# Folding the second attention's weights inside the first expert layer's routing, and mixing expert rows on VectorE

## The reference, cut to what matters

```
x = x + tanh(g_ffn[0])   * L0_ffn(layernorm(x))      # 64 experts, top 3
x = x + tanh(g_xattn[1]) * L1_xattn(layernorm(x))    # 16 heads of 64

L0_ffn:  logits = x @ gate_w + gate_b;  top 3, gates = softmax(top 3)
         pos = running count of tokens per expert;  valid = pos < 64
         buf[expert, pos] = x
         y = gelu(buf @ w1 + b1) @ w2 + b2            # per expert
         out[token] = sum over k of y[expert_k, pos_k] * gate_k * valid_k
L1_xattn: q = x @ Wq; k = ctx @ Wk; v = ctx @ Wv
         out = softmax(q k^T / 8) v, heads joined, @ Wo + bo
```

## Time and profile before

| | us |
|---|---|
| median of 3 runs | 4144.75 |
| lowest and highest run | 4140.34, 4147.81 |
| profiled execution, its own time | 4137.59 |
| its span in the profile | 4136.0 |
| mean granted TensorE clock | 0.924 |

### The profile page before, as it was taken

The page is one execution under the profiler, slowest core; times in us unless marked ns, Lnnn a source line. Parts: engine busy times, 40 slices in busy tenths (PEclk is TensorE's granted clock), DMA queues, the critical chain, the costliest instruction groups (busy, mean ns, idle before and its releaser), DMA issues. The chain is left out here.

```text
span 4136.0 us, 84598 instructions
## 1 busy us (share of the span) xinstructions
PE 3638.2 (88%) x33128; PEld 2481.3 (60%) x33128; DVE 2430.1 (59%) x3802; ACT 2047.4 (50%) x2959; POOL 1527.6 (37%) x1887
## 2 busy tenths in 40 slices
PE   8499999946489999989999997679958799999997
PEld 8367777733366666666666665257733366666664
DVE  7556666543245554515454542467644799999993
ACT  8177777711134443434443442166422377777764
POOL 5265545221423233213323220022201577666651
PEclk9699999968789999999999997889969699999998
DMA  6177777546223332213333220021000566666650
GB/s 188 49 170 178 176 167 175 145 182 235 52 71 90 84 91 81 80 51 87 81 87 87 83 78 26 10 64 46 13 19 16 123 145 144 140 140 147 145 120 15
DMA packets 202294, 421.94 MB, mean 102 GB/s; under 512 B 51993, under 2 KB 108244, under 8 KB 201844
## 3 DMA queue, kind: packets, MB, share of 16 engines
q1 hardware_dynamic: 131524, 327.92, 31.2%
q0 software_dynamic: 34944, 46.10, 5.1%
q10 hardware_dynamic: 35504, 43.39, 3.9%
HBM read 232.39 MB, written 32.56 MB: 64 GB/s over the span
## 5 line engine op out<-in xcount | busy, mean ns | idle before, releaser
L1512 DVE TENSOR_REDUCE L_mp<-ps 128x2 f32<-128x1000 f32 (+1 forms) x352 | 402.4, 1151 | 560.7 <-PE ps L1310 557.3
L1347 PE MATMUL ps<-L_p,L_cn 125*97 125x448 f32 x1536 | 639.2, 538 | 0.0
L1494 ACT ACTIVATE L_p<-ps 125x896 f32<-125x896 f32 x384 | 352.1, 917 | 533.8 <-PE ps L1335 462.5
L2291 DVE TENSOR_REDUCE L_mp<-ps 112x1 f32<-112x500 f32 x726 | 454.2, 667 | 64.5 <-PE ps L2040 64.4
L1333 PE MATMUL ps<-L_qh,L_ch 97*125 97x448 f32 x768 | 384.4, 501 | 0.0
L1347 PEld LDWEIGHTS ps<-L_p,L_cn 125*97 125x97 f32 x1536 | 250.4, 163 | 199.9 <-issue 165.9
L2241 ACT ACTIVATE L_p<-L_p 125x896 f32<-125x896 f32 x256 | 243.3, 950 | 178.6 <-DVE L_p L2308 178.0
L2308 DVE TENSOR_SCALAR L_p<-ps 125x896 f32<-125x896 f32 x256 | 276.5, 1080 | 24.6 <-PE ps L2061 24.5
L920 ACT ACTIVATE L_p<-ps,rk 125x896 f32<-125x896 f32 x256 | 257.7, 1007 | 50.9 <-PE ps L776 46.8
L1334 PE MATMUL ps<-L_ql,L_ch 96*125 96x448 f32 x768 | 282.3, 368 | 0.0
L1335 PE MATMUL ps<-L_qh,L_cl 96*125 96x448 f32 x768 | 280.8, 366 | 0.0
(11 more groups left out here) (538 smaller groups left out, 7632.6 us busy)
## 6 DMA issues: line engine op xcount, KB each, us to landing
L_ks<-L_k_part SPq DMA_DIRECT2D x288, 375.0 KB, 6.1
L_ks<-L_k_first SPq DMA_DIRECT2D x96, 375.0 KB, 5.2
moe_w<-in_L_w SPq DMA_DIRECT2D x64, 512.0 KB, 6.6
L_cn<-in_ctxN SPq DMA_DIRECT2D x32, 568.4 KB
cs_ct<-in_ctxT SPq DMA_DIRECT2D x32, 562.5 KB, 4.2
L_cr<-in_ctxT POOLq DMA_DIRECT2D x32, 562.5 KB
L_ch<-in_ctxT POOLq DMA_DIRECT2D x32, 562.5 KB, 4.5
L_raw<-in_ctxT SPq DMA_DIRECT2D x32, 562.5 KB, 5.1
```

The source lines that it names most:

```text
L1347: mm = nc.tensor.matmul(U[:, a, :], CN[s][:, j, :], P[:, n % 2, a * HALF:(a + 1) * HALF], start=(j == 0), stop=(j == KT - 1))
L1494: nc.scalar.activation(two(P[:, n % 2, :]), SB[n % 2], ACT.Exp).then_inc(S["exped"].sem, 1)
L1512: nc.vector.tensor_reduce(mp[:, 2 * k:2 * k + n], ps[:, bank:bank + n, 0:500], AX.X, ALU.max).then_inc(S["chunk_maxed"].sem, 1)
L2291: nc.vector.tensor_reduce(mp[:, 2 * c + a:2 * c + a + 1], ps[0:TT, CB[0].start + a, 0:500], AX.X, ALU.max).then_inc(S["chunk_maxed"], 1)
```

## The change

The fold block goes. `M`, `N` and `cq` are allocated before `experts0` and filled inside its routing block. The L1 weights are loaded into the last two of the 14 expert slots, which are not yet loaded: WqT and WkAT on partitions 0 to 63 of `moe_w1` and `moe_w2`, Wo and WvA on partitions 64 to 127. SP issues these five loads after the gate loads and before the zero stores; it loads the last two slots' expert weights only after `folded` has reached 5. PE does the fold and the cq columns after its 14 turns and before it waits for `routed` and counts. ACT copies the folded banks to `M` and `N` and scales cq, ahead of its three exponentials. The layer norm `a1` runs without loads beside it.

In the mixing block the diagonals and their matmuls go. When a group's rows have landed, DVE multiplies them with the gates and adds them up (five instructions a group, in `mix`), PE turns the sum (14 transposes in all), and DVE adds it to `xT` (in `add`). DVE does `add(g)` before `mix(g + 1)`.

```diff
-def fold_weights(core, L, M, N, cq, scale, keep_max, dh, values, norm=None):
...
-def attention_wide(core, L, src, bo, scale, bit, image, norm):
+def attention_wide(core, L, src, bo, scale, bit, image, folded, held):
...
-        fold_weights(core, L, M, N, cq, scale, True, 64, None, norm)
...
+FOLD_BANKS = (6, 2, 4, 6)
...
+            def unfolded(t, p, n):
+                return t[p:p + DH1, NS - 2:NS, :, :].rearrange("p s e n -> p (s e n)")[:, 0:H * n].rearrange(
+                    "p (h n) -> p h n", n=n)
+            wqt, wka = unfolded(w1, 0, D), unfolded(w2, 0, KA)
+            wo, wva = unfolded(w1, DH1, D), unfolded(w2, DH1, KA)
...
+                    for dst, name in ((wqt, "WqT"), (wka, "WkAT"), (wo, "Wo"), (wva, "WvA"), (bqh[:, :], "bqh")):
+                        sp.dma_start(dst, d[f"L1_{name}"]).then_inc(S["fold_in"], 16)
                     sp.wait_ge(S["zeroed"], 1)
...
                     for s in range(NS):
+                        if s == NS - 2:
+                            sp.wait_ge(S["folded"], 5)
                         load_weights(sp, s, s)
...
+                    pe.wait_ge(S["fold_in"], 80)
+                    pe.wait_ge(S["rows_copied"], 1)
+                    for g in range(4):
+                        if g == 3:
+                            pe.wait_ge(S["fold_placed"], 2)
+                        for k in range(4):
+                            h = 4 * g + k
+                            nc.tensor.matmul(ps[:, FOLD_BANKS[g], k * KA:(k + 1) * KA], wqt[:, h, :], wka[:, h, :],
+                                             start=True, stop=True)
+                            mm = nc.tensor.matmul(ps[0:KA, FOLD_BANKS[g] + 1, k * D:(k + 1) * D], wva[:, h, :],
+                                                  wo[:, h, :], start=True, stop=True)
+                        mm.then_inc(S["folded"], 1)
+                    pe.wait_ge(S["fold_placed"], 4)
+                    for h in range(H):
+                        mm = nc.tensor.matmul(ps[0:KA, FOLD_BANKS[1], h:h + 1], wka[:, h, :], bqh[:, h:h + 1],
+                                              start=True, stop=True)
+                    mm.then_inc(S["folded"], 1)
                     pe.wait_ge(S["routed"], 1)
...
+                    for g in range(4):
+                        act.wait_ge(S["folded"], g + 1)
+                        nc.scalar.activation(M[:, 4 * g:4 * g + 4, :].rearrange("p h n -> p (h n)"),
+                                             ps[:, FOLD_BANKS[g], 0:4 * KA], ACT.Copy).then_inc(S["fold_placed"], 1)
...
+                    act.wait_ge(S["folded"], 5)
+                    nc.scalar.activation(cq[:, :], ps[0:KA, FOLD_BANKS[1], 0:H], ACT.Copy, scale=scale)
                     act.wait_ge(S["exp_in"], 1)
...
+                    def mix(g):
...
+                        dve.wait_ge(S[f"gathered{g}"], 16 * TOPK0 * len(tiles))
+                        nc.vector.tensor_tensor(mixed[:, u, :], yr[0][:, u, :], gates(0), ALU.mult)
...
-                                mm = nc.tensor.matmul(ps[:, g, (t % 4) * TT:(t % 4 + 1) * TT], yr[k][:, t, :],
-                                                      by_gate[k][:, t, :], start=(k == 0), stop=(k == TOPK0 - 1))
+                            mm = nc.tensor.transpose(ps[:, g, (t % 4) * TT:(t % 4 + 1) * TT], mixed[:, t, :],
+                                                     core.ident[:, :])
...
-        attention_wide(core, "L1", core.xn, v(core, "L1_bo"), 0.125, bit, image, norm1)
+        layer_norm(core, core.xT, core.xn, "a1")
+        attention_wide(core, "L1", core.xn, v(core, "L1_bo"), 0.125, bit, image, folded, held)
```

More of the change, by code:

```diff
@@ L437 @@
 QV = H // 4 * NQ
-def fold_weights(core, L, M, N, cq, scale, keep_max, dh, values, norm=None):
[L442 to L502, removed]
-                if keep_max:
-                    dve.wait_ge(m_mm.sem, 2)
-                    nc.vector.tensor_scalar(cq[:, :], ps[0:KA, 0, 0:H], scale, None,
-                                            ALU.mult).then_inc(m_sb.sem, 1)
@@ L2420, in experts0 @@
     C4 = HID0 // 128
+    M, N, cq = folded
+    DH1 = 64
     with ExitStack() as ctx:
@@ L2752, in experts0 @@
             yr = [sb(f"yr{k}", [TT, NT, D], c=c3) for k in range(TOPK0)]
-            by_gate = [sb(f"by_gate{k}", [TT, NT, TT], c=c3) for k in range(TOPK0)]
+            mixed = sb("mixed", [TT, NT, D], c=c3)
+            part = sb("part", [TT, 2, 4, D], c=c3)
             groups = [range(g, min(g + 4, NT)) for g in range(0, NT, 4)]
             S = {n: core.sig(f"moe_{n}").sem for n in [f"gathered{g}" for g in range(len(groups))]
-                 + ["gates_act", "gates_dve", "mix_turned"]}
+                 + ["mixed", "mix_turned"]}
             with nc.Block() as block:
@@ L2766, in _, with gates, add @@
                                     bounds_check=R - 1, oob_is_err=False).then_inc(S[f"gathered{g}"], 16)
-                @block.scalar
-                def _(act):
-                    for t in range(NT):
-                        nc.scalar.activation(by_gate[0][:, t, :], core.ident[:, :], ACT.Copy,
-                                             scale=gat[0][:, t:t + 1]).then_inc(S["gates_act"], 1)
                 @block.vector
                 def _(dve):
-                    for t in range(NT):
-                        for k in range(1, TOPK0):
-                            nc.vector.tensor_scalar(by_gate[k][:, t, :], core.ident[:, :], gat[k][:, t:t + 1], None,
-                                                    ALU.mult).then_inc(S["gates_dve"], 1)
-                    for g, tiles in enumerate(groups):
+                    link = core.linker(dve, "dve")
+                    def mix(g):
+                        tiles = groups[g]
+                        u = slice(tiles[0], tiles[-1] + 1)
+                        def gates(k):
+                            return gat[k][:, u].unsqueeze(2).to_broadcast([TT, len(tiles), D])
+                        dve.wait_ge(S[f"gathered{g}"], 16 * TOPK0 * len(tiles))
+                        nc.vector.tensor_tensor(mixed[:, u, :], yr[0][:, u, :], gates(0), ALU.mult)
+                        for k in (1, 2):
+                            ins = nc.vector.tensor_tensor(part[:, k - 1, 0:len(tiles), :], yr[k][:, u, :], gates(k),
+                                                          ALU.mult)
+                        link(ins)
+                        link(nc.vector.tensor_tensor(mixed[:, u, :], mixed[:, u, :], part[:, 0, 0:len(tiles), :], ALU.add))
+                        nc.vector.tensor_tensor(mixed[:, u, :], mixed[:, u, :], part[:, 1, 0:len(tiles), :], ALU.add
+                                                ).then_inc(S["mixed"], 1)
+                        dve.wait_ge(S["mixed"], g + 1)
+                    def add(g):
+                        tiles = groups[g]
+                        s = slice(tiles[0] * TT, (tiles[-1] + 1) * TT)
                         dve.wait_ge(S["mix_turned"], g + 1)
-                        s = slice(tiles[0] * TT, (tiles[-1] + 1) * TT)
                         nc.vector.scalar_tensor_tensor(
@@ L2785, in _ @@
                             in1=core.xT[:, s], op0=ALU.mult, op1=ALU.add)
+                    for g in range(len(groups)):
+                        mix(g)
+                        add(g)
                 @block.tensor
```

26 lines of the change are left out of this document (12 added, 14 removed).

## The result

The changed kernel took 4119.0 us (median of 4 runs, 4116.28 to 4119.56) beside 4143.26 us for the kernel before in the same comparison: ratio 0.9939, 95% interval 0.9922 to 0.9956, or 24.3 us less (18.2 to 32.3). Over all runs of the two kernels, 78 of the kernel before have their median at 4141.8 and 9 of the changed one at 4119.6: 22.2 us. The forecast was 19.0 us, and 4125.7 us as the time. The first comparison lies past the forecast's own bounds (15 to 22.7 us, 4122 to 4130); the second lies inside the bounds for the gain.

What follows compares the result with a forecast made beforehand. TensorE was busiest at 88%, but the bounds named were the routing's count, the mixing's last landing and the fold alone. Terms -19.9 + 1.5 - 0.6 = -19.0 us took 4144.75 to 4125.7 us; the forecast's own bounds were 4122 to 4130.

Steps and rivals of the forecast that it cites:

- The fold block, -19.9: At the first queries: the fold block, from 1139.97 to 1159.82, disappears whole, saving 19.9 us.
- The fold in the routing, +1.5: In the routing: fold and cq ahead of the count move its end from 896.3 to near 897.7, +1.5 us.
- the price of a head: Fold in the routing: one head's M and N matmuls, overlapping on different row halves, take 0.50 us at half clock.
- cq, 3.5 us: Fold in the routing: the cq columns take 3.5 us, between 5.4 at half clock and 2.7 at full.
- The course of the clock: In the routing: PE reaches full clock after 5 us and loses it during cq; alternatives gave -1.6 or +5.6 us.
- The mixing, -0.6: In the mixing: last group's tail -0.5, gathers freed of diagonals -0.4, new products slowing others +0.3; -0.6 us.
- gathers above 1.1 us: In the mixing: gathers longer than 1.1 us beside products were named as a sign that the forecast is wrong.
- The rival of full exclusion: In the mixing: products and additions hold up POOL's gathers, last landing 9.8 us later; 4135.6 us, chance 0.08.
- The layer norm, 0: At the layer norm: losing the loads beside it is worth nothing, as it was a chain of its own engines.
- The halves don't overlap: In the routing: heads take 12.8 us at half clock, count ends 10.4 us later; 4134.6 us, chance 0.20.
- PE's signal comes late: In the mixing: second group's signal at 1120.7 delays the end to 1129.9 from 1123.1; 4133.1 us, chance 0.17.
- Weights late: In the routing: fold weights land with queued loads at 918.7, count ends 37.7 us late; 4162 us, chance 0.04.

Runs made afterwards that it cites:

- same_half: Changed kernel with both weight pairs of the fold on partitions 0 to 63, Wo and WvA in slots 10 and 11; 4130.52 us, 0.9969 of the kernel before.
- fold_twice: Changed kernel with the fold's 32 matmuls in the routing issued twice into the same places; 4124.17 us, 0.9951 of the kernel before.
- busy_wide: Changed kernel plus 4 unused matmuls of 512 columns ahead of the transposes of mixing groups 0 to 2; 4122.34 us, 0.9954 of the kernel before.
- psum_mix: Changed kernel with the mixing's running sum in PSUM, three 128x128 instructions a tile instead of five wide ones a group; 4117.99 us, 0.9939 of the kernel before.
- busy_pe: Changed kernel plus 12 unused matmuls of 128 columns ahead of the transposes of mixing groups 0 to 2; 4133.11 us, 0.9974 of the kernel before.

## Why the prediction was right or wrong

*The fold block, -19.9:* the profiled pair shows 19.85. But the execution that the sum rested on had part of that block at full clock. Two other executions of the same block took 21.07 us (21.58 from the norm's end), so the term is -19.85 to -21.07, -20.65 as a mean of the three. **This is a step that failed in size:** one profiled execution stood for the kernel.

*The fold in the routing, +1.5:* the mechanism was right (two halves at once, weights in time, cover up to the count), the size was not, and by the most. **The failed terms** are the price of a head, 0.50 us at half clock from the expert pairs of the earlier trace rows, where 0.43 was measured (0.22 at full clock), and cq, 3.5 us as a mean of two levels, where 2.8 was measured, since the granted clock was 1.0 there. In the prediction the fold and cq end at 882.4 + 10.3 = 892.7, 2.2 us behind the masks; in the first execution they ended 0.2 us ahead of them, so DVE set the count's start. The course of the clock was a guess: full clock after 5 us, lost again during cq. Neither execution followed it: in the first, about the first five heads, the last two and all of cq had full clock, in the second cq alone. The row behind the guess, 0.85 in the layer norm, was one execution, and the same norm had 0.62 in the next. The count took 4.8 us in place of 5.75, since part of it had full clock; at half clock nearly throughout it takes 6.1 to 6.2 (`same_half`, `fold_twice`, `busy_wide`), so the prediction's 5.8 was already a mixed price. The routing changed by -0.9 or +0.5 us depending on the clock, -0.25 on average over eight executions with this fold.

*The mixing, -0.6:* +0.4 in the first pair, -0.2 to -0.8 if the mean of the executions with the new one (62.0 us from first gather to last addition) is set against two or three with the old (61.5, 62.8, 64.1). Its parts were off: the tail gained 0.5, as predicted, but the gathers lost 1.0 where -0.1 was forecast. The row that misled is the 1.14 us beside the diagonals; beside the new products a gather takes up to 0.5 us longer, and gathers above 1.1 us were one of the prediction's own signs of being wrong. The rival of full exclusion (9.8 us) was far too strong: 3.3 us of such instructions a group delayed the gathers by 0.3 to 0.65 us. The rule of the Trainium skill behind that rival (SBUF — State Buffer, SBUF: two separate sides) would block a gather for the whole of an instruction; the trace differs, with 1.00 us for a gather beside the first product (1074.71 above). That the lengthening went with `psum_mix` fits the pair that the rule names, but the width changed with it.

*The layer norm, 0:* not refuted, and not shown. The first pair has +1.9, the means above have +0.8 over few executions of two distinct lengths.

The sum with these means is -20.65 - 0.25 - 0.2 to -0.8, -21.1 to -21.7, or up to 0.8 less with the norm's means. Against it stand 22.2 us between the medians of all runs, and 24.3 and 19.6 in the two comparisons. So the terms account for about 2 us more than the forecast, most of it in the routing; the intervals of the two comparisons overlap, and what lies between them isn't traced to any stretch. Against the median of the nine runs the time was off by 6.1 us: 3.2 us of gain, and 3.0 us because the median of three runs, 4144.75, lies that much above the median of all.

*The rivals.* "The halves don't overlap" was priced at 4134.6; `same_half` shows it, at 4130.5. "PE's signal comes late" did not happen, yet the mechanism is real: `busy_pe` has it, with 12.1 us behind the gathers where 6.8 was priced. It did not happen because 4 records a group are too few. The prediction's reason, that PE's work in a group is now a fifth, points the right way, but `busy_wide` shows that the number of records counts and not the work. "Weights late" did not happen: the fold waited for ACT's copy.

## What to carry to other kernels

Work that depends on weights alone belongs into a stretch where TensorE waits for VectorE; measure that wait, since what is longer than it comes back one for one, and put the two operand pairs on different halves of the rows, which took 0.52 of the time here. Read a short stretch in more than one execution before pricing it: the same code differed here by 1 to 2.5 us in four of five stretches. Don't put trains of short matmuls beside a train of indirect DMAs when someone waits for their signal; four long ones delayed no signal here, though they cost their own time.

## What the runs showed of the hardware that was not expected

- TensorE's signals beside indirect gathers came late by 7 and 17 us with 28 short records in quick succession, by 4 to 21 us in two groups with the 24 of the old mixing, by up to 1.5 us with 12, by 0.1 us with 4, and by 0.1 us with 12 long ones.
- Beside VectorE instructions of 512 columns with two SBUF operands some gathers took 1.14 to 1.54 us instead of 1.00, others 1.00 to 1.03; beside instructions of 128 columns with the running sum in PSUM all stayed at 1.00 to 1.03.
- With matmuls on 64 rows each, on different halves, in PE's idle time, the granted clock of the routing stretch was 0.65 in five executions and 0.54 in three, where it had been 0.50 in the three without a fold there; in `same_half`, with as many matmuls on one half, it stayed at 0.50. In the eight, the cq columns ran at 0.90 to 1.00, and in seven of them the count took 4.8 to 5.0 us where it had taken 5.8.
